# First context loads moved into the cell stage, attend one unit later, and edge work of the wide attention's heads reordered

## The reference, cut to what matters

```python
x = x + _L0_xattn_ref(_layernorm(x), ctx, ctx, mask, ...)    # 16 heads, masked      "mask" stage
x = x + _L0_attn_ref(_layernorm(x), L0_attn_context, ...)    # 8 heads of 128, 1024 keys  "wide"
x = x + _L0_ffn_ref(_layernorm(x), ...)                      # a cell of 6 attention nodes "cell"
x = x + _L1_xattn_ref(_layernorm(x), ctx)                    # softmax(q @ ctx.T) @ ctx    "ctx"
x = x + _L1_attn_ref(_layernorm(x), ...)                     # a scan                "scan"
x = x + _L1_ffn_ref(_layernorm(x), ...)                      # a feed-forward        "ffn"
```

## Time and profile before

| | |
|---|---|
| median of 3 runs | 3028.55 us (3021.83 to 3031.35) |
| the profiled execution | 3023.51 us, its span 3021.8 us |
| mean granted TensorE clock | 0.981 |
| busy, share of the span | PE 94%, PEld 73%, DVE 72%, ACT 67%, POOL 39% |
| wide stage, from the trace | about 577 to 1524 us |
| cell stage | about 1529 to 2579 us |
| context stage | about 2584 to 2701 us |

### The profile page before, as it was taken

How to read it: one execution, slowest core, us unless ns; L and a number is a source line. 1 busy time by engine, 2 the same in 40 slices (tenths; PEclk the granted TensorE clock), 3 DMA queues, 4 the chain that set the end, 5 groups by cost and what they waited for, 6 DMA issues and landing times. The chain is left out here.

```text
span 3021.8 us, 84584 instructions
## 1 busy us (share of the span) xinstructions
PE 2846.0 (94%) x32038; PEld 2212.3 (73%) x32038; DVE 2163.7 (72%) x5328; ACT 2032.1 (67%) x4128; POOL 1177.9 (39%) x962
## 2 busy tenths in 40 slices
PE   8999999789999999999889999999999998789999
PEld 6888888556666666666577887887888787456798
DVE  7888888777777767776536778777778776568443
ACT  6888888787777777777606766676667666333444
POOL 6777777576565565565501001011010000111210
PEclk9999999999999999999989999999999999899899
DMA  4111111267677787788961112111111110761000
GB/s 149 52 58 57 53 61 36 39 135 143 145 159 155 145 155 148 147 162 155 209 196 54 37 44 72 37 44 55 37 44 51 51 37 20 284 224 44 8 21 29
DMA packets 616893, 283.51 MB, mean 94 GB/s; under 512 B 548971, under 2 KB 593958, under 8 KB 614326
## 3 DMA queue, kind: packets, MB, share of 16 engines
q1 hardware_dynamic: 596630, 235.35, 32.5%
q10 hardware_dynamic: 19968, 44.05, 4.2%
HBM read 123.59 MB, written 21.50 MB: 48 GB/s over the span
## 5 line engine op out<-in xcount | busy, mean ns | idle before, releaser
L1479 POOL TENSOR_TENSOR front_parts<-front_prob,front_parts 128x1024 f16<-128x1024 f32 x256 | 545.9, 2133 | 360.6 <-ACT front_parts L1687 334.1
L1675 ACT ACTIVATE front_prob<-wide_score,wide_neg_max,front_s_up 128x1024 f32<-128x1024 f32 x256 | 307.5, 1201 | 147.5 <-DVE wide_neg_max L1778 142.2
L1775 DVE TENSOR_REDUCE wide_row_max<-wide_score 128x1 f32<-128x1024 f32 x256 | 312.5, 1221 | 124.8 <-PE wide_score L1520 124.5
L1520 PE MATMUL wide_score<-wide_kT,wide_qT 128*128 128x512 f16 x1536 | 375.3, 380 | 6.8 <-ACT front_prob L1675 5.3
L2071 POOL TENSOR_TENSOR cell_w<-cell_w_stage,cell_w 128x1536 fp32r<-128x1536 f32 x23 | 80.5, 3502 | 641.3 <-ACT cell_w L2339 641.3
L790 POOL TENSOR_TENSOR common_common<-common_common,mask_inv_sum 128x512 f32<-128x512 f32 x256 | 272.3, 1064 | 107.9 <-DVE mask_inv_sum L1188 105.3
L1687 ACT ACTIVATE front_parts<-front_prob 128x1024 f16<-128x1024 f32 x256 | 269.9, 1054 | 29.7 <-issue 10.9
L1045 ACT ACTIVATE common_common<-common_common,mask_row_min 128x256 f32<-128x256 f32 x512 | 254.7, 502 | 48.0 <-DVE mask_row_min L1136 47.8
L1520 PEld LDWEIGHTS wide_score<-wide_kT,wide_qT 128*128 128x128 f16 x1536 | 144.4, 98 | 154.5 <-ACT front_prob L1675 7.3
L2533 DVE TENSOR_REDUCE cell_row_max<-cell_score 128x8 f32<-128x512 f32 x192 | 131.2, 683 | 156.8 <-PE cell_score L2169 154.7
L1136 DVE CUSTOM_DVE_ANT_0 common_common<-mask_score,front_prob 128x256 f32<-128x256 f32 x512 | 189.2, 417 | 3.5 <-issue 3.5
(11 more groups left out here) (349 smaller groups left out, 6606.3 us busy)
## 6 DMA issues: line engine op xcount, KB each, us to landing
cell_w_stage<-cell_weights ACTq DMA_DIRECT2D x24, 768.0 KB, 5.2
front_cT<-in_ctx_turned SPq DMA_DIRECT2D x32, 512.0 KB, 3.3
ctx_ctx<-in_ctx_odd SPq DMA_DIRECT2D x16, 1024.0 KB, 7.3
cell_w_stage<-in_L_ffn_W_own ACTq DMA_DIRECT2D x24, 512.0 KB, 3.6
common_common<-in_L_ffn_W_pairs SPq DMA_DIRECT2D x18, 512.0 KB, 4.5
front_prob<-in_mask_BxS_ik SPq DMA_DIRECT2D x32, 256.0 KB, 3.5
front_probT<-front_parts SPq DMA_TRANSPOSE x512, 2.8
ctx_ctx<-in_ctx_even SPq DMA_DIRECT2D x16, 512.0 KB, 5.8
```

The lines of the kernel that those rows point to most:

```text
L1479: pool.tensor_tensor(parts[:, s % 2, LO, :], prob[:, s % 2, :], parts[:, s % 2, HI, :], ALU.subtract).then_inc(part_lo, 1)
L1520: mm = pe.matmul(score[:, s % 2, half * 512:(half + 1) * 512], qT[:, u_par, a, s * P:(s + 1) * P], kT[:, par, b, half * 512:(half + 1) * 5 ...
L1675: act.activation(prob[:, s % 2, :], score[:, s % 2, :], ACT.Exp, bias=neg_max[:, s % 2:s % 2 + 1], scale=s_up[:, 0:1], accum_out=row_sum[: ...
L1775: dve.tensor_reduce(row_max[:, one], score[:, s % 2, :], AX.X, ALU.max).then_inc(max_found, 1)
```

## The change

Four parts.

1. Wide stage, edges. In "split" ACT splits the weights at s = 0 instead of 1, and DVE takes its two halves at s = 0 and s = 1 instead of both at s = 1. In "keys" both engines split the weights at s = 0 instead of 2. In both, ACT's `output_hi` for the second half comes ahead of the exp at s = 3 instead of behind it.
2. Wide stage, SP. The eight weight pairs are loaded in 32 pieces of 128 KB, one a unit, in units 24 to 55 (heads 3 to 6), instead of one a unit in the last head. The stage waits for the first six stores of x alone; the last two are waited for in the cell stage, by SP ahead of its ninth weight pair and by ACT ahead of its first copy.
3. Context stage, loads. Input rows and context of the first eight units are loaded by SP in the cell stage's last round (three batches: after slots (3,0) and (3,1) and at node 4's end), into places that the cell stage no longer needs. The wait for the cell's last stores moves to the context stage's SP, ahead of its first own load. The new object `ContextFront` has a clear of its own, and it and `CellFront` end behind the context stage: one clear stands between cell and context where two did, three between context and scan where one did.
4. Context stage, order. `attend`, `finish` and `store` run for unit u-2 in step u; the reciprocal (`invert`) stays at u-1. Loads so wait for a unit that is finished a step later.

```diff
--- before.py
+++ after.py
@@ -581,9 +581,20 @@
...
         self.act_sb = mem.sb("act_w", [P, NODES])
+        self.PIECE = 2 * MAT // self.PIECES
         self.raw_places = [self.common[:, rows(x * 2 * MAT, 2 * MAT)] for x in range(self.RAW)]
+        self.x_stored = mem.sem("x_stored")
         self.w_loaded = mem.sem("w_loaded")
...
+    def load_piece(self, sp, m):
+        n, part = m // self.PIECES, rows(m % self.PIECES * self.PIECE, self.PIECE)
+        sp.dma_start(self.raw_places[n][:, part], self.sources[2][n][:, part]).then_inc(self.raw_loaded[n], 16)
+    def loaded(self, n):
+        return 16 * (n // self.RAW + self.PIECES)
...
@@ -594,6 +605,52 @@
...
+class ContextFront:
+    NBUF = 8
...
+            self.home = Memory(mem.nc, early, mem.stage).sb("home", [P, 2, 2, NODES, DH, BLK])
+        self.node = mem.sb("node", [P, 2, 2, NODES, DH, BLK], mybir.dt.float32r)
...
+    def load_rows(self, sp, u, k):
+        sp.dma_start(self.x_sb[:, k, :], self.x_in[rows(u * P, P), :]).then_inc(self.x_loaded[k], 16)
+    def load_context(self, sp, n, k):
...
+            sp.dma_start(self.piece(k).rearrange("p (t d) -> p t d", d=D),
+                         self.ctx_even[rows(n, 1)].rearrange("u p (t d) -> p (u t) d", d=D)).then_inc(self.ctx_loaded[k], 16)
...
+            sp.dma_start(self.home[:, X, :, at].rearrange("p a h c -> p a (h c)"),
+                         self.ctx_odd[rows(n, 1)].rearrange("u p (a c) -> p (u a) c", a=2)).then_inc(self.ctx_loaded[k], 16)
...
@@ -1438,24 +1496,25 @@
...
                 front.weights(sp, pair + 1, par)
-            if h == HEADS - 1:
-                cell_front.load_pair(sp, n)
-                if n == 0:
+            m = u - (UNITS - NBLK - cell_front.RAW * cell_front.PIECES)
+            if 0 <= m < cell_front.RAW * cell_front.PIECES:
+                cell_front.load_piece(sp, m)
+                if m == 0:
                     cell_front.load_small(sp)
-                if n >= 2:
-                    store(n - 2)
-        def store(n):
+            if h == HEADS - 1 and n >= 2:
+                store(n - 2, y_stored)
+        def store(n, stored):
             sp.wait_ge(y_added, n * 2 + ((HEADS - 1) * NBLK + 1) * 2)
-            sp.dma_start(block_rows(x_out[n * BLK:(n + 1) * BLK, :]), x_all[:, n * SUB:(n + 1) * SUB, :]).then_inc(y_stored, 16)
+            sp.dma_start(block_rows(x_out[n * BLK:(n + 1) * BLK, :]), x_all[:, n * SUB:(n + 1) * SUB, :]).then_inc(stored, 16)
...
                 unit(h // 2, h % 2, n, n % 2, "close" if n == NBLK - 1 and h + 1 < HEADS else "mid")
+        sp.wait_ge(y_stored, 16 * (NBLK - 2))
         for n in (NBLK - 2, NBLK - 1):
-            store(n)
-        sp.wait_ge(y_stored, 16 * NBLK)
+            store(n, cell_front.x_stored)
...
@@ -1691,6 +1750,8 @@
...
             for s in range(SUB):
+                if edge in ("split", "keys") and s == 3:
+                    output_hi(u * 2 - 1, 1)
                 if s + 1 < SUB:
...
@@ -1699,7 +1760,7 @@
...
                     query_hi(u + 1, 1 - u_par)
-                if edge != "first" and s == 3:
+                if edge not in ("first", "split", "keys") and s == 3:
                     output_hi(u * 2 - 1, 1)
...
@@ -1709,14 +1770,14 @@
...
                     output_hi(u * 2 - 2, 0)
+                if edge == "split" and s == 0:
+                    act.wait_ge(w_loaded[1 - par], (pair + par + 1) * W_LOADS)
+                    front.scalar_kv_weights_hi(act, 1 - par)
+                if edge == "keys" and s == 0:
+                    weights_hi(h + 1, 1 - par)
                 if edge in KV_AT and s < 2:
...
                     kv_hi_part(1 - par, i, misc_ps[:, :], (h + 1) * KV + i + 1)
-                if edge == "split" and s == 1:
-                    act.wait_ge(w_loaded[1 - par], (pair + par + 1) * W_LOADS)
-                    front.scalar_kv_weights_hi(act, 1 - par)
-                if edge == "keys" and s == 2:
-                    weights_hi(h + 1, 1 - par)
...
@@ -1801,17 +1862,17 @@
...
                     query_lo(u + 1, 1 - u_par)
+                if edge == "keys" and s == 0:
+                    weights_lo(h * 2 + 4, 1 - par)
                 if edge != "first" and s == 1:
                     output_lo(u * 2 - 2, 0)
+                if edge == "split" and s < 2:
+                    front.vector_kv_weights_lo(dve, h * 2 + 3 + s, 1 - par, s)
                 if s == 1 and ahead is not None and ahead + 1 < NBLK:
...
                     kv_lo_part(1 - par, i, misc_ps[:, :], (h + 1) * KV + i + 1)
-                if edge == "split" and s == 1:
-                    front.vector_kv_weights_lo(dve, h * 2 + 4, 1 - par)
-                if edge == "keys" and s == 2:
-                    weights_lo(h * 2 + 4, 1 - par)
                 if edge != "first" and s == 3:
...
@@ -2060,6 +2120,19 @@
...
+        i = ITER - 1
+        sp.wait_ge(proj_ready, proj_at(i, 3, 0) + PROJ_SLOT)
+        for k in range(ahead.NBUF):
+            ahead.load_rows(sp, k, k)
+        for k in (0, 2, 3):
+            ahead.load_context(sp, k // 2, k)
+        sp.wait_ge(proj_ready, proj_at(i, 3, 1) + PROJ_SLOT)
+        for k in (1, 5):
+            ahead.load_context(sp, k // 2, k)
+        sp.wait_ge(acc_ready, (attention(i, 4, 1) + 1) * DH)
+        for k in (4, 6, 7):
+            ahead.load_context(sp, k // 2, k)
...
@@ -2367,6 +2440,7 @@
...
+        act.wait_ge(front.x_stored, 32)
         copy_input(0, 0)
...
@@ -2626,17 +2698,15 @@
...
-def stage_context_attention(nc, mem, const, x_in, ctx_even, ctx_odd, x_out):
+def stage_context_attention(nc, mem, const, front, x_out):
...
     UNITS = TOK // PAIR
-    NBUF = 8
+    NBUF = front.NBUF
     KT = CTX // P
...
-    x_sb = mem.sb("x", [P, NBUF, D])
-    HALF = 2 * KT * D
-    ctx_both = mem.sb("ctx", [P, NBUF // 2, 3 * HALF])
+    x_sb, even = front.x_sb, front.even
     stats = mem.sb("stats", [P, 2, 6])
...
@@ -2723,20 +2787,17 @@
...
     def _(sp):
-        def load(u, k, i=None):
-            if not isinstance(u, int) or u >= NBUF:
-                sp.wait_ge(y_ready, u - NBUF + 1)
-            sp.dma_start(x_sb[:, k, :], x_in[rows(u * PAIR, PAIR), :]).then_inc(x_loaded[k], 16)
-            at, wide, source = (0, HALF, ctx_even) if even(k) else (HALF, 2 * HALF, ctx_odd)
-            n = u // 2 if isinstance(u, int) else i * (NBUF // 2) + k // 2
-            sp.dma_start(ctx_both[:, k // 2, at:at + wide], source[rows(n, 1)].rearrange("u p c -> p (u c)")).then_inc(ctx_loaded[k], 16)
-        for k in range(NBUF):
-            load(k, k)
+        def load(u, k, n):
+            sp.wait_ge(y_ready, u - NBUF + 1)
+            front.load_rows(sp, u, k)
+            front.load_context(sp, n, k)
+        for X in range(2):
+            sp.wait_ge(front.x_stored[X], 16 * (NBLK // 2))
         with sp.Fori(1, UNITS // NBUF) as i:
             for k in range(NBUF):
-                load(i * NBUF + k, k, i)
+                load(i * NBUF + k, k, i * (NBUF // 2) + k // 2)
...
@@ -2814,11 +2875,12 @@
...
                 turn_unit(u + 1, (k + 1) % NBUF)
-            if exists(u, k, -1):
-                attend(u - 1, (k - 1) % NBUF)
+            if exists(u, k, -2):
+                attend(u - 2, (k - 2) % NBUF)
...
             turn_probs(UNITS - 1, NBUF - 1)
+            attend(UNITS - 2, NBUF - 2)
             attend(UNITS - 1, NBUF - 1)
...
@@ -2933,7 +3001,9 @@
...
             if exists(u, k, -1):
-                finish(u - 1, (k - 1) % NBUF)
+                invert(u - 1, (k - 1) % NBUF)
+            if exists(u, k, -2):
+                finish(u - 2, (k - 2) % NBUF)
             if exists(u, k, 2):
...
@@ -3469,10 +3544,14 @@
...
                     stage_wide_attention(nc, Memory(nc, ctx, "wide"), const, front, cell_front, x[1])
-            with ExitStack() as ctx:
-                stage_cell(nc, Memory(nc, ctx, "cell"), const, cell_front, x[1], *of("L0_ffn_", "W_own ln_g ln_b"), x[2])
-        with ExitStack() as ctx:
-            stage_context_attention(nc, Memory(nc, ctx, "ctx"), const, x[2], a["ctx_even"], a["ctx_odd"], x[3])
+            with ExitStack() as both:
+                shared = Memory(nc, both, "ahead")
+                ahead = ContextFront(shared, x[2], a["ctx_even"], a["ctx_odd"])
+                both.callback(shared.clear)
+                with ExitStack() as ctx:
+                    stage_cell(nc, Memory(nc, ctx, "cell"), const, cell_front, ahead, x[1], *of("L0_ffn_", "W_own ln_g ln_b"), x[2])
+                with ExitStack() as ctx:
+                    stage_context_attention(nc, Memory(nc, ctx, "ctx"), const, ahead, x[3])
         with ExitStack() as both:
...
```

77 lines of the change are left out of this document (51 added, 26 removed).

## The result

The changed kernel takes 2985.48 us in the median of four runs (2983.91 to 2987.70), the kernel before 3025.19 in four (3020.22 to 3031.35). The ratio is 0.9868, with an interval of 0.9846 to 0.9891: faster by 1.1 to 1.5%. The profiled execution has a span of 2982.2 us against 3021.8, so 39.6 us are to be found between the two traces. The forecast was 2990.5 with 2976 to 3006.

The account below looks back on a forecast made before the run. PE was taken as the wide stage's bound (busy 900.72 of 947 us), so only its idle time could be won. 19.3 + 7.4 - 1.0 + 2.6 + 7.1 = 35.4 us gave 2990.5, range 2976 to 3006.

Parts of the forecast that it names:

- Keys: Wide stage's keys units: weights moved behind `wide_qT` fill DVE's hole; saves 7.3 us in heads 1 to 6, 5.0 in head 0.
- Split: Wide stage's split units: `output_hi` ahead of the exp helps; saves 6.8 us in heads 1 to 6, 0.2 in head 0.
- Rival 1: Split units: POOL still blocks the second half and the stall stays; gain 28.4 us, time 2997.5, chance 0.18.
- Last head: Wide stage's last head: without pair loads, 4.9 of 7.9 us excess goes, plus 2.5 of the last unit's wait, together 7.4.
- Half stays: Wide stage's last unit: half of PE's 4.99 us wait for turned probabilities stays, 2.5 goes.
- Pieces: Wide stage: 32 pieces in SP's queue among units at the bound, charged 1.0 us; a quarter of 0.6 each would be 4.8.
- Rivals 2 and 3: Wide stage: each piece costs 0.6 us (time 3008.7, chance 0.06); pieces block the turns, 1.5 us a unit (3037, chance 0.02).
- Seams: Between stages: wide to cell gains 2.6 us, cell to context 5.8, two more clears cost 1.4; chain to first scores stays.
- Context stage: 15 pairs gain 0.15 us each, 2.3; 1.0 added for a start without 7 MB queued, 0.6 off for the tail.
- Rival 4: Context stage: loads six units ahead make odd units' scores wait 1 us for each of 12 loads; time 3005, chance 0.06.

Follow-up runs that it names:

- only the order: The changed kernel with the weight splits of the edges back in their old places, `output_hi` still ahead of the exp: 3001.41 us, ratio 0.9926 to the kernel before.

## Why the prediction was right, and where not

**Keys: right, by its mechanism.** The forecast was 12.3 and 13.2 came. The reason (an op on SBUF operands held until POOL's is done, the hole behind `wide_qT`) is what the runs on order, place and POOL's length show. The 0.9 over it is that the units went below the close unit's 15.87, the bound I took.

**Split: right.** 7.0 forecast, 7.9 measured. That the second half would be only 0.3 us earlier was close (0.4: it ends 0.28 behind POOL's op instead of 0.67), and so was the weight on `output_hi`: the order alone brings 6.2 of 7.2. Rival 1 is out, since its block stayed and its stall did not.

**Last head: the sign right, the size wrong.** "Without the load I charge each of the five the 0.6 that one 512 KB transfer cost in the second" failed. The 0.6 of that one unit was taken for the price of any transfer, and a store alone costs 0. The reading under it, that the third to seventh unit "have both", was wrong for the third: it lost its 1.7 before the first store was issued. The second unit's 0.6 was no price of a pair either. SP issued the three small loads behind that pair, and the same unit took 13.24 in the variant with the pairs put back, where the third lost 1.8. So all of the excess hangs on the pairs and goes with them: 12.5 instead of 7.4, beside the upper bound of 12.9. What a pair costs by itself at a unit's end, from 0.06 to 1.8, stays open. "Half stays" of the last unit's wait failed alike: 4.99 became 0.83.

**Pieces: the bound by the close units was right.** 1.0 charged; in the traces the 0 to 1.1 of unit 27 was paid, and whatever of units 34 and 35 is due to them. Rivals 2 and 3, a price by number and turns held up, are out: in the changed kernel the mid units from 36 on take 13.16 to 13.19, with pieces in all of them up to the last head. One variant (the first eight units loaded late) shows two units, 42 and 43, of 13.7.

**Seams: right within 0.5 us each.** Wide to cell 2.4 for 2.6; cell to context 5.4 for 5.8; two more clears 0.9 for 1.4. The chain to the first scores gained 1.2 that I had at zero: PE's mean clock from the first turn to the scores is 0.71 instead of 0.61, after an idle time of 11.58 us instead of 17.01. With late loads it is 0.72 after 15.04. In the variants that leave this part alone the chain takes 7.3 to 8.6, with the longest (8.56, "only the order") at a clock of 0.58 after 11.89. So the idle time does not order them, much of the 1.2 is scatter between executions, and the cause stays open.

**Context stage: wrong by 5.1 us.** "0.15 a pair, 15 pairs, 2.3" is right for a pair without a stall (6.11). The step that failed is "I add 1.0 for a stage that no longer starts with 7 MB in its queues", with the waits for y's stores not carried over at all. No term stood for them: the landing of y's stores (4.2 us in the median before, 7.2 at most) was not set against the time after which a place comes round. That time is two units, 6.1 us, and landings reach 7.6, so each pair stands near a stall, and four places remove all of them (92.55). The size of the miss is that of one execution: in the nine traces with this stage the pairs take 96.6 to 101.0. Rival 4 looked for the loss at the loads; it came from the stores.

Two errors of 5.1 each, in the last head and in the context stage, cancelled, by luck. So the sum of 35.4 stands near the traces' 39.6 by its reasons in part 1 and the seams alone.

## What to carry to other kernels

Where a DVE op on SBUF tensors is longer than its kind, look for a GpSimd op that ends just before it, and move it behind that op or into a stretch where nobody waits for DVE. Price transfers by what stands in the queue ahead of the ones that are waited for, and in every unit, not in one: the same 512 KB load cost 0.06 us in one unit, 1.8 in the next and nothing in the middle of a unit, so move it, and leave its size alone. Before a price is laid on two transfers together, see which of them had been issued when the engine waited. Before shortening a loop, compare the time after which each buffer comes round with the longest landing of its store, not the median: here twice the places for y gave the stage 6 us, and the reordering with two places nothing that can be told.

## What the runs showed that was not expected

- The end of a held DVE op is fixed: 0.28 us after POOL's, at 1230.94, 1240.19 and in head 0 at 692.27, though the ops themselves are 0.48 long in their old place under a short POOL op.
- A unit that began as a 512 KB load landed, at a DMA share of 1.05, lost nothing, while units with a share of 0.93 and 0.94 lost 1.3 and 1.8 us. The share does not tell whether a transfer hurts.
- A wait of 2.85 us in the context stage made a pair 3.7 us longer: PE's granted clock over that pair was 0.84, and eight matmuls of the attend take 1.98 us behind the stall (at 2630.61) and 1.09 before it.
- Executions differ by some 3 to 6 us each in units 34 and 35, the cell stage, the start of the wide stage and the pairs of the context stage; what lies behind units 34 and 35 was not tested.
